# Score units by head in a masked attention, earlier gathers, and a router that splits fewer expert weights

## The reference

```python
x = x + tanh(g_xattn[0]) * L0_xattn(layernorm(x), ctx, ctx, ...)         # 16 heads of 16, rotary positions
x = x + tanh(g_ffn[0])   * L0_ffn(layernorm(x), gate_w, gate_bias, ...)  # 8 experts, 2 per token, and a shared one
x = x + tanh(g_xattn[1]) * L1_xattn(layernorm(x), ctx, ctx, mask, ...)   # 16 heads of 64, a mask
x = x + tanh(g_ffn[1])   * L1_ffn(layernorm(x), ...)                     # 8-bit rounded activations and weights

# L1_xattn
scores = einsum('bhqd,bhkd->bhqk', q, k) / sqrt(64)
scores = where(mask == 0, -1e9, scores)
out = einsum('bhqk,bhkd->bhqd', softmax(scores), v)
return merge_heads(out) @ W_o + b_o

# L0_ffn
scores = softmax(xt @ gate_w.T)
_, indices = top_k(scores + gate_bias, 2)
combine = (one_hot(indices, 8) * take_along_axis(scores, indices, 1)[..., None]).sum(1)
y = sum over e of mlp(xt, w1[e], w2[e], w3[e]) * combine[:, e:e+1]
return y + mlp(xt, sw1, sw2, sw3)
```

## Time and profile before

| what | us |
|---|---|
| median of three runs | 2144.2 |
| profiled execution, its own time | 2143.8 |
| profiled execution, span from first to last instruction | 2141.7 |
| PE busy | 1743.6 (81%) |
| DVE busy | 1415.4 (66%) |
| ACT busy | 1103.9 (52%) |
| POOL busy | 1034.0 (48%) |

### The profile page before, as it was taken

How to read it: one execution, slowest core, us unless ns; L and a number is a source line. 1 busy time by engine, 2 the same in 40 slices (tenths; PEclk the granted TensorE clock), 3 DMA queues, 4 the chain that set the end, 5 groups by cost and what they waited for, 6 DMA issues and landing times. The chain is left out here.

```text
span 2141.7 us, 45574 instructions
## 1 busy us (share of the span) xinstructions
PE 1743.6 (81%) x14369; PEld 1163.1 (54%) x14375; DVE 1415.4 (66%) x2938; ACT 1103.9 (52%) x2568; POOL 1034.0 (48%) x1543
## 2 busy tenths in 40 slices
PE   0588888886258979999995899999999999998376
PEld 0344444443234546666663676767676767776123
DVE  4356667675975434444444787778787877877796
ACT  1266666664632212222221666666666666666776
POOL 1555555550735732232315666666666666554004
PEclk9689999998569999999997999999999999999697
DMA  3000000000820011222213222222232332320102
GB/s 104 12 9 12 10 10 10 10 5 1 267 78 1 1 47 57 69 71 63 79 44 94 70 73 70 69 72 69 74 78 69 78 77 70 79 63 11 41 1 79
DMA packets 89345, 117.62 MB, mean 55 GB/s; under 512 B 16520, under 2 KB 58768, under 8 KB 89232
## 3 DMA queue, kind: packets, MB, share of 16 engines
q1 hardware_dynamic: 76176, 90.08, 15.6%
q0 software_dynamic: 6528, 17.83, 3.0%
q10 hardware_dynamic: 6528, 8.39, 1.2%
HBM read 56.36 MB, written 17.83 MB: 35 GB/s over the span
## 5 line engine op out<-in xcount | busy, mean ns | idle before, releaser
L1069 POOL TENSOR_SCALAR a_P<-a_P,a_RS 128x256 f32<-128x256 f32 x512 | 254.5, 497 | 235.4 <-DVE a_RS L1351 206.1
L1238 ACT ACTIVATE a_P<-a_pS,a_NM 128x256 f32<-128x256 f32 x512 | 237.9, 471 | 198.3 <-DVE a_NM L1347 194.6
L815 DVE TENSOR_REDUCE a_M<-a_pS 128x2 f32<-128x512 f32 x256 | 164.6, 685 | 142.6 <-PE a_pS L626 142.3
L1247 ACT ACTIVATE a_PH<-a_pT 128x512 f16<-128x512 f32 x256 | 154.1, 602 | 80.5 <-PE a_pT L1163 70.5
L1347 DVE TENSOR_REDUCE a_NM<-a_pS 128x2 f32<-128x512 f32 x256 | 174.7, 682 | 26.3 <-PE a_pS L1155 20.7
L1357 DVE TENSOR_TENSOR a_PL<-a_pT,a_PH 128x512 f16<-128x512 f32 x256 | 172.5, 674 | 16.9 <-ACT a_PH L1247 16.8
L754 ACT ACTIVATE a_PT<-a_pT 128x512 f32<-128x512 f32 x256 | 139.0, 597 | 71.4 <-PE a_pT L645 71.1
L1163 PE MATMUL a_pT<-g_ident,a_P 128*128 128x128 f32 x1024 | 155.9, 275 | 19.9 <-POOL a_P L1069 19.9
L1163 PEld LDWEIGHTS a_pT<-g_ident,a_P 128*128 128x128 f32 x1024 | 120.0, 141 | 38.2 <-POOL a_P L1069 19.3
L1946 ACT ACTIVATE me_hh<-me_pH 128x512 f16<-128x512 f32 x72 | 43.0, 597 | 175.7 <-PE me_pH L1933 175.7
L99 PE MATMUL a_pF<-a_ch,xw_XW 128*128 128x256 f16 x512 | 103.1, 285 | 32.2 <-DVE a_VL L1339 29.2
(11 more groups left out here) (442 smaller groups left out, 5251.9 us busy)
## 6 DMA issues: line engine op xcount, KB each, us to landing
a_KD<-a_KN SPq DMA_DIRECT2D x128, 128.0 KB, 2.3
a_QS<-a_QN SPq DMA_DIRECT2D x128, 128.0 KB, 2.3
mr_stage<-mw SPq DMA_DIRECT2D x24, 512.0 KB, 4.7
ys<-me_yb SPq DMA_DIRECT2D x72, 128.0 KB, 1.7
a_ctxin<-ctxT SPq DMA_DIRECT2D x32, 256.0 KB, 2.7
a_KZ<-a_KN SPq DMA_DIRECT2D x64, 128.0 KB, 2.3
g_X<-x SPq DMA_DIRECT2D x1, 4096.0 KB, 15.1
rows<-mr_row ACTq DMA_DIRECT2D x32, 128.0 KB, 3.6
```

The costliest lines, as they stand in the source:

```text
L815: nc.vector.reduce_max(M[:, :, a, p2], pS[a][:], AX.X).then_inc(s_max.sem, 1)
L1069: last = nc.gpsimd.tensor_scalar(P32[u % 4][:, a, :], P32[u % 4][:, a, :], RS[u % 4][:, a:a + 1], LIFT, ALU.mult, ALU.mult)
L1238: last = nc.scalar.activation(P32[u % 4][:, a, :], pS[u % 2][:, a, :], ACT.Exp, bias=NM[u % 4][:, a:a + 1], accum_out=SM[u % 4][:, a:a + 1])
L1247: nc.scalar.activation(PH[p2 % 2][:, :, :, j * P:(j + 1) * P].rearrange("p a k q -> p (a k) q"), pT[u % 2][:].rearrange("p a k q -> p (a k ...
```

## The change

Three parts. In the second attention a unit becomes one head and all 256 queries; the scores of a pair's two heads are one block on PE that fills both `pS` banks, and the low-key products contract over 64 rows, the two heads on the two halves of the array's rows. `KZ` and its zero fills go. The keys come first in a front, the normalised input's transposes move to turn 6, the front's turns are laid out anew. In the first batch all gathers are issued at once, the folding of the value bias into the output bias moves beside the front, in turn 12.

In the router only the first nine matrices are split, all on POOL and in quarters of the columns; ACT normalises; SP stores. The other 18 are split in the shared expert, by halves, ACT rounding and POOL subtracting. There DVE builds the patterns, four pairs at a time, and routing steps stand behind a step's low part.

```diff
@@ attention1
-    HALF = [START + i * 2 // 3 for i in range(24)]
-    KEYS, QUERIES, VALUES = HALF[0:8], HALF[8:16], HALF[16:24]
+    KEYS, QUERIES, VALUES = ([start + i * 2 // 3 for i in range(8)] for start in (2, 8, 13))
+    NORMAL, TURNED = 4, 6
...
-        run(UNITS, comb(0, 0, 0))
-        run(UNITS, now(front(0, 0)), comb(1, 1, 0))
+        run(UNITS, at_once(comb(0, 0, 0)), now(front(0, 0)), beside, comb(1, 1, 0))
+        filled()
...
-                        sp.dma_start(KD2[par][a][0:64, pr, :], KN[0][r, pr, :]).then_inc(stacked[half].sem, 16)
-                        sp.dma_start(KD2[par][a][64:P, pr, :], KN[0][r, pr, :]).then_inc(stacked[half].sem, 16)
-                        sp.dma_start(KZ[par][a][0:64, pr, :], KN[1][r, pr, :]).then_inc(stacked[half].sem, 16)
+                        sp.dma_start(KD2[par][a][0:64, pr, :], KH[r, pr, :]).then_inc(stacked[half].sem, 16)
+                        sp.dma_start(KD2[par][a][64:P, pr, :], KH[r, pr, :]).then_inc(stacked[half].sem, 16)
...
-            for z in (z for zs in KZ for z in zs):
-                nc.gpsimd.memset(z[64:P, :, :], 0.0).then_inc(cleared, 1)
-            pool.wait_ge(cleared, 5)
...
-                def scores(u):
-                    p2, j = u // 2, u % 2
-                    if u == 0:
+                def scores(p2):
+                    if p2 == 0:
                         masks.wait(pe, b, 1)
...
-                    e_ready.wait(pe, b, u - 1) if u or not isinstance(b, int) or b else None
-                    out = pS[u % 2]
-                    nc.tensor.matmul(out[:], identb[:], maskq[par][:, j:j + 1, :].broadcast_to([P, 2, S]), start=True, stop=False)
+                    e_ready.wait(pe, b, 2 * p2)
                     for a in range(2):
-                        q = QS[par][a][:, p2, j * P:(j + 1) * P]
-                        nc.tensor.matmul(out[:, a, :], q, KD2[par][a][:, p2, :], start=False, stop=False)
-                        last = nc.tensor.matmul(out[:, a, :], q, KZ[par][a][:, p2, :], start=False, stop=(a == 1))
-                    last.then_inc(s_full.sem, 1)
+                        nc.tensor.matmul(pS[a][:], identb[:], maskq[par][:], start=True, stop=False)
+                        for j in range(2):
+                            nc.tensor.matmul(pS[a][:, j, :], QS[par][a][:, p2, j * P:(j + 1) * P], KD2[par][a][:, p2, :], start=False, stop=False)
+                    for j in range(2):
+                        for a in range(2):
+                            r = slice(64 * a, 64 * a + 64)
+                            last = nc.tensor.matmul(pS[a][:, j, :], QS[par][a][r, p2, j * P:(j + 1) * P], KL[par][r, p2, :], start=False, stop=(j == 1))
+                            if j == 1:
+                                last.then_inc(s_full.sem, 1)
...
-                return plan(*[(u, lambda u=u: scores(u)) for u in range(UNITS)],
+                return plan(*[(2 * p2, lambda p2=p2: scores(p2)) for p2 in range(PAIRS)],
                             *[(u + LAG_T, lambda u=u: transposes(u)) for u in range(UNITS)],
...
-            batches(pe, uncombined, front, back)
+            batches(pe, uncombined, front, back, plan((12, fold)))
@@ moe_router
+            for j in range(NS):
+                load(j)
+            for t in range(TILES):
+                store(t)
+                if t % 4 == 3 and NS + t // 4 < len(jobs):
+                    load(NS + t // 4)
...
+                pool.wait_ge(staged[j % NS], 16 * (j // NS + 1))
+                for a in range(PIECES):
+                    cols = slice(a * PIECE, (a + 1) * PIECE)
+                    nc.gpsimd.tensor_copy(hi[:, cols], stage[j % NS][:, cols]).then_inc(w_hi, 1)
+                for a in range(PIECES):
+                    cols = slice(a * PIECE, (a + 1) * PIECE)
+                    pool.wait_ge(w_hi, PIECES * j + a + 1)
+                    nc.gpsimd.tensor_tensor(lo[:, cols], stage[j % NS][:, cols], hi[:, cols], ALU.subtract).then_inc(w_lo, 1)
...
+                nc.scalar.activation(xn[t % 2][:], X[:, t, :], ACT.Identity, bias=nb[:, t:t + 1], scale=rstd[:, t:t + 1]).then_inc(xn_ready.sem, 1)
@@ moe_shared
+            for n, (src, hi, lo) in enumerate(halves):
+                pool.wait_ge(w_hi, n + 1)
+                for cols in (slice(0, F0 // 2), slice(F0 // 2, F0)):
+                    nc.gpsimd.tensor_tensor(lo[:, cols], stage[n % 2][:, cols], hi[:, cols], ALU.subtract).then_inc(w_lo, 1)
...
             for g in range(STEPS):
                 silu(g)
+                if g and 2 * g - 2 < len(halves):
+                    weight_high(2 * g - 2)
                 high(g)
+                if g and 2 * g - 2 < len(halves):
+                    weight_high(2 * g - 1)
...
                 hidden(g)
-                routing(g)
                 if g >= FK and g % FK == 0:
                     for t in range(g - 4, g):
                         result(t)
                 low(g)
+                routing(g)
@@ moe
+    NOW = 9
...
+        moe_router(nc, c2, X, mean, rstd, XT, gw_d, gb_d, gb, rows_d, L, consts, jobs[:NOW])
...
+        moe_shared(nc, c2, X, XT, W["w1"], W["w3"], W["w2"], consts, gb, L, POS, GW, ETAB, IDS, jobs[NOW:])
```

More of the change, by code:

```diff
@@ L922, in attention1 @@
     q_hi, q_lo = s.counter("q_hi", 4), s.counter("q_lo", 4)
-    stacked = [s.counter(f"stacked{half}", 160) for half in range(2)]
+    stacked = [s.counter(f"stacked{half}", 128) for half in range(2)]
     v_hi, v_lo = s.counter("v_hi", 4), s.counter("v_lo", 4)
@@ L953, in now, with at_once, batches @@
         return {t: p[t] for t in p if t < UNITS}
-    def batches(eng, comb, front, back):
+    def at_once(p):
+        return plan(*[(0 if t < ROOT else 1, do) for t in sorted(p) for do in p[t]])
+    def batches(eng, comb, front, back, beside={}, filled=none):
         def step(new, old, *soon):
@@ L1305, in normalised @@
                     if not isinstance(b, int) or b:
-                        f_full.wait(dve, b, 1 - f_full.per)
+                        f_full.wait(dve, b, 5 - f_full.per)
                     for j in range(2):
@@ L1381, in back @@
                             *[(2 * p2 + LAG_PV, lambda p2=p2: out_low(p2)) for p2 in range(PAIRS)], (END, finish), (END + 1, statistics))
-            batches(dve, comb, front, back)
+            batches(dve, comb, front, back, plan((1, biases)), fold)
             measured.wait(dve, B, 0)
@@ L1412, in _, with load, store @@
             sp.dma_start(gin[:], gw_d.rearrange("(k p) n -> p k n", p=P)).then_inc(gate_in, 16)
-            for j, (src, hi, lo) in enumerate(jobs):
+            sp.dma_start(gb[:], gb_d.partition_broadcast(P)).then_inc(gb_in, 16)
+            def load(j):
+                src, hi, lo = jobs[j]
                 if j >= NS:
-                    sp.wait_ge(w_lo, j - NS + 1)
+                    sp.wait_ge(w_lo, PIECES * (j - NS + 1))
                 sp.dma_start(stage[j % NS][:].rearrange("p (a b) -> p a b", a=src.shape[1]), src).then_inc(staged[j % NS], 16)
+            def store(t):
+                lo_ready.wait(sp, t, 1)
+                sp.dma_start(rows[t, :, :], row[t % NR][:].rearrange("p a d -> p (a d)")).then_inc(stored[t % NR].sem, 16)
+            for j in range(NS):
[4 more added lines that the diff above has]
+                    load(NS + t // 4)
+            sp.wait_ge(gb_in, 16)
+            for q in range(NR):
+                stored[q].wait(sp, TILES // NR, 0)
         @block.gpsimd
@@ L1462, in high @@
                 nc.scalar.activation(row[t % NR][:, 0, :], xn[t % 2][:], ACT.Copy).then_inc(hi_ready.sem, 1)
[L1464 to L1466 removed]
             def logits(t):
                 l_full.wait(act, t, 1)
[L1470 to L1475 removed]
+                nc.scalar.activation(L[:, t, :], pL[t % NL][:], ACT.Copy).then_inc(l_out.sem, 1)
+            act.wait_ge(nb_ready, 1)
+            normalise(0)
             high(0)
+            normalise(1)
             high(1)
             for t in range(TILES):
[L1480 to L1482 removed]
                 if t + 2 < TILES:
+                    normalise(t + 2)
                     high(t + 2)
[L1485 to L1487 removed]
+                if t:
+                    logits(t - 1)
+            logits(TILES - 1)
         @block.tensor
```

297 lines of the change are left out of this document (158 added, 139 removed).

## The result

The changed kernel takes **2342.3 us** in the median of four runs (2339.2 to 2344.7); the kernel before, run beside it, 2144.6 (2143.4 to 2149.2). The ratio is 1.0914 (95% interval 1.0891 to 1.0937): 9% slower. The profiled execution took 2341.7 us (span 2339.9), 198.2 us more span than before. The forecast was 2295 with a range of 2200 to 2345.

A forecast was written before the change was run, and what follows sets the result against it. In the second attention PE's throughput was nearly the bound, DVE close behind; the change adds a loop of waits. 2143.8 + 120 (loop) + 9 (last batch) + 61 (clock) - 9 (batch 0) - 35 (router) + 5 (shared expert) = 2295 us, range 2200 to 2345.

The forecast's parts named there:

- The wait and its loop: Second attention: score blocks wait for the odd unit's late exponentials; 58.7 us a batch, +120 us over fifteen batches (104 to 150).
- The clock: Second attention: PE's idle waits bring half-clock stretches, four waits a batch x 0.6 x 1.7 us, +61 us (0 to 102).
- The score block: Second attention: a pair's score block on PE goes from 1.32 to 1.28 us, two 64-row products a slot, two shape changes.
- Rival 4: Second attention: 64-row products do not overlap in this order of banks; +26 us, total 2321; chance 0.05.
- The shared expert: Shared expert: weight halves fit in ACT's wait, patterns move from POOL to DVE; +5 us (-20 to +24).
- The router: Router: tile period falls from 2.33 to 1.2 us; -35 us (-41 to -23).
- The ends: First batch with its gathers -9 us (0 to -14); last batch, from the loop, +9 us (0 to 13).
- the three small terms: Router -35 us, batch 0 and the gathers -9 us, last batch +9 us.
- rival 3: Second attention: every idle stretch of PE costs the clock; total 2336 us; chance 0.10.
- Rival 2: Second attention: the loop binds but the clock holds; total 2234 us; chance 0.20.
- Rival 1: Second attention: the loop does not bind, odd exponentials end before PE's next block; total 2100 us, faster; chance 0.10.

The follow-up runs named there:

- two kernels with early maxima: Changed kernel with both units' maxima taken in turn 2p on DVE: alone 2162.6 us; with both units' exponentials early on ACT too, 2101.1 us.
- The filled waits: Changed kernel with twelve unread 256-column products on PE ahead of the score blocks of pairs 4 to 7: 2292.9 us.
- all weights in the router: Kernel with both maxima and exponentials early, but all 27 weight matrices split in the router, none in the shared expert: 2163.7 us in one run.
- both maxima and exponentials early: Changed kernel with both units' maxima on DVE and exponentials on ACT moved to turn 2p, ahead of that turn's evictions: 2101.1 us.
- The old units, paired: New router and shared expert with the old second attention, its scores, maxima and exponentials of both units in turn 2p: 2115.7 us.
- patterns before the low part: Both maxima and exponentials early, identity products a step later, DVE's patterns before its low part in the shared expert: 2094.4 us; with third staging buffer 2093.2.

## Why the prediction was right, and where it was off

**The wait and its loop: right.** The prediction named the wait for the odd unit, what is queued behind it, and why the odd maximum is late. The predicted pairs sum to 58.7 us a batch; the shortest ones after (7.26 taken for pair 2, whose 7.0 stands in batch 0) sum to 6.32 + 5.65 + 7.26 + 7.91 + 8.38 + 8.03 + 8.30 + 7.58 = 59.4, which is 131 us over fifteen batches for the 120 predicted, well inside 104 to 150. The two kernels with early maxima show it as cause: with one of the two cuts pairs 3 and 4 are those that the working gives for it (pair 5 is 0.3 us longer), and with both the wait is gone.

**The clock: right, a little small.** 201.3 - 131 = 70 us for the 61 predicted. In batches 1 to 14 it is 43 stretches / 14 = 3.1 a batch, at some 1.5 us each; the prediction had 4 waits x 0.6 = 2.4 at 1.7. The chance taken from the earlier trace rows, three of five waits, was near: 38 of the 56 waits ahead of pairs 3 to 6 were followed by such a stretch (0.68). The other 5 stand behind the 14 waits ahead of pair 7, which the sum left out. By the measure of the earlier trace rows these waits are 1.8 to 3.2 us long, and length alone does not decide: in every second batch pair 4's wait of 3.2 us was not followed by a stretch at 0.50, and pair 6's of 2.4 us was. The filled waits show the cause.

**The score block: right.** 1.30 us where 1.28 was predicted. PE's timeline after, from one block's first product to the work behind it:

```profile
1745.65 0.39 PE L1151 MATMUL a_pS<-a_maskq,g_identb 128*128 128x512 bf16 x1 [0.40 <-ACT a_P L1244]
...
1746.31 0.38 PE L1153 MATMUL a_pS<-a_KD,a_QS 128*128 128x256 f16 x2
1746.62 0.39 PE L1157 MATMUL a_pS<-a_KL,a_QS 64*128 64x256 f16 x4
1746.95 0.28 PE L99 MATMUL a_pF<-a_ch,xw_XW 128*128 128x256 f16 x1
```

1746.31 to 1746.62 is two slots of 0.11 and 0.09; 1746.62 to 1746.95 is two slots for four products and 0.11. The change of shape is there on both sides, as taken from the earlier trace rows. Rival 4 falls.

**The shared expert: the step that failed.** "0.60 us of ACT each between silu and high part, which fits in ACT's wait" and half a subtraction in front of DVE's steps only as the worst case: I took +5, it is +21.7, near that worst case (24). The halves do fit into ACT; what they bring with them, POOL's subtractions, makes DVE's own operations longer (11 us more busy time than without them), and DVE's patterns and low part are what PE waits for (16.8 and 13.9 us in the changed kernel, 13.4 and 7.1 with all weights in the router). The 23 us of PE's idle time were not to be had either: with the patterns on DVE, PE waits longer for them than it did for POOL's (8.8). The earlier trace rows had shown it, DVE standing behind POOL in the router; the mean should have been nearer the bound. How much of the 15 to 19 us is DVE's own time and how much the clock (granted clock 0.90 in the changed kernel's shared expert, 0.95 with all weights in the router) was not parted.

**The router: right.** -31.9 for -35: a tile takes 1.32 us (537.2 to 578.0 by 31, the last row below), predicted 1.2. ACT's normalising was taken at 0.41 us and takes 0.59; DVE's low part still meets POOL (0.55 in the median, up to 0.94). ACT's and DVE's parts, count, ns min/median/max, first and last start; they answer to the earlier trace rows.

```profile
L1487 ACT ACTIVATE mr_xn<-g_X,mr_nb,g_rstd x32: 584/588/602, 536.1 to 577.0; 128x256 f32<-128x256 f32 x32
L1494 ACT ACTIVATE mr_row<-mr_xn x32: 416/416/418, 536.7 to 577.6; 128x256 f16<-128x256 f32 x32
L1467 DVE TENSOR_TENSOR mr_row<-mr_xn,mr_row x32: 424/554/944, 537.2 to 578.0; 128x256 f16<-128x256 f32 x32
```

**The ends: inside their bounds, the last one by luck.** First batch -5.8 (0 to -14), last batch +12.9 (0 to 13). Neither was tried by itself. But the loop, from which the working took the last batch's +9, is only some 3 of the 12.9: with both maxima and exponentials early 217.5 us are left, 10.0 above the 207.5 before. The old units, paired, have 212.2, 3 to 5 us more than the unpaired ones (209.0 beside the new router, 207.5 before), so a part of the 10 comes with the paired order; the rest stays open.

**The sum.** Of the 47 us between 2295 and 2342, 17 are the shared expert, 20 the loop and its clock, 10 the three small terms. All missed on the same side, so the result lies at the range's upper edge, 3 us inside it; that it lies inside at all is luck. In size it is near rival 3 (2336), but the clock, that rival's whole difference, is only 9 us of the 47. Rival 2 fell with the clock. Rival 1 did not happen in this kernel. It is what the early maxima and exponentials make true, and its 2100 us is their 2101, though by other terms: the fifteen batches are 30 us shorter than that sum has them (-35 for -5), the shared expert 14 longer, the last batch, where the sum has no term, 10.

## What to carry to other kernels

When one wait comes to stand for two units of work, ask for the later one when its first step is issued, on every in-order queue between it and the wait: here both the maximum on DVE and the exponentials on ACT were a turn late behind evictions, and two short edits of the plan were worth 241 us. Waits of 1.8 to 3.2 us on the matrix engine were paid a second time in the granted clock in 43 of 70 cases; filling them with products that nobody reads shows the price. Work on engines that have room is not free: splitting 18 matrices on ACT and POOL cost 15 to 19 us of the shared expert, and DVE's operations beside POOL's 53 us of subtractions were 11 us longer.

## What the runs showed that was not expected

- The best versions (early maxima and exponentials, patterns before the low part, with two or three staging buffers) take 2094 and 2093 us, 2.3 to 2.4% less than the kernel before, with all of the change in them.
- Four 64-row products take two slots whether the heads alternate or not (batches of 48.4 and 48.5 us).
- 768 added products made a kernel 49 us faster, since they held the granted clock.
- One kernel, that with the fillers, stopped PE for up to 2.0 us five times, 9.0 us in all, at the end of a batch, with no other engine named; six other profiles have no such stop in these batches, and the cause wasn't sought.
- The router, with its code unchanged, took 36.9 to 41.0 us in ten single profiles and 51.4 in one. Differences of a few us between these kernels are therefore not told apart.
